# A graph network's edge passes: a third one-hot buffer, gathers one block further ahead, 64 landing counters

## What is computed

```python
x = x + _L0_gnn_ref(h, ..., src, dst)            # sum over edges of H[src] * norm
x = x + _L1_gnn_ref(h, edge_attr_20, edge_weight, src, dst, ...)
x = x + _L2_gnn_ref(h, src, dst, ...)            # 4 rounds: segment_max of message(src)
x = x + _L3_gnn_ref(h, edge_index, ...)          # 2 rounds: segment_sum
...
msg = h[src] * norm[:, None]
out = jax.ops.segment_sum(msg, dst, num_segments=n_nodes)
```

## Time and profile before

| what | value |
|---|---|
| runs | 11399.97, 11347.6, 11393.48 us; median 11393.48 us |
| the profiled execution | 11520.23 us |
| its span, first to last instruction | 11518.5 us |
| mean granted TensorE clock | 0.822 of full |
| busy TensorE / VectorE / GpSimd | 8143.9 / 5554.7 / 6674.3 us |

### The profile page before, as it was taken

How to read it: one execution, slowest core, us unless ns; L and a number is a source line. 1 busy time by engine, 2 the same in 40 slices (tenths; PEclk the granted TensorE clock), 3 DMA queues, 4 the chain that set the end, 5 groups by cost and what they waited for, 6 DMA issues and landing times. The chain is left out here.

```text
span 11518.5 us, 121592 instructions
## 1 busy us (share of the span) xinstructions
PE 8143.9 (71%) x34932; PEld 4146.4 (36%) x35457; DVE 5554.7 (48%) x11902; ACT 820.8 (7%) x2270; POOL 6674.3 (58%) x6440
## 2 busy tenths in 40 slices
PE   4777748888757776677757777477774777667774
PEld 2333237777733332333332333233322333233331
DVE  4455434444445554444545554455544554445554
ACT  2000021111130000100000000100001000010000
POOL 4555568888835555555555555555555555555555
PEclk8888867777778888888878888788887888878887
DMA  4333435555532222222222222222223222322223
GB/s 166 124 129 128 139 88 77 77 77 76 67 106 84 85 85 86 78 80 84 84 81 82 81 85 82 74 85 85 85 84 95 84 85 83 94 79 84 84 83 104
DMA packets 580217, 1042.14 MB, mean 90 GB/s; under 512 B 149064, under 2 KB 419250, under 8 KB 525900
## 3 DMA queue, kind: packets, MB, share of 16 engines
q0 software_dynamic: 298368, 418.22, 17.3%
q1 hardware_dynamic: 278650, 620.49, 15.5%
q10 hardware_dynamic: 2940, 1.00, 0.0%
HBM read 492.11 MB, written 555.62 MB: 91 GB/s over the span
## 5 line engine op out<-in xcount | busy, mean ns | idle before, releaser
L997 POOL DMA_INDIRECT WORK<-table,stage x5124 | 4904.5, 957 | 4178.1 <-DVE WORK L1102 2412.7
L1145 PE MATMUL bank<-TF,XF 128*128 128x512 bf16 x16800 | 5594.1, 414 | 2073.2 <-issue 1029.5
L1080 DVE TENSOR_TENSOR TF<-AF,bank 128x3584 bf16<-128x3584 bf16 x1225 | 2472.3, 2018 | 3645.1 <-remote 2758.8
L1145 PE MATMUL bank<-TF,Z 128*128 128x512 bf16 x8400 | 3467.4, 413 | 181.0 <-issue 176.0
L1145 PEld LDWEIGHTS bank<-TF,XF 128*128 128x128 bf16 x17150 | 1742.5, 104 | 4604.4 <-issue 1902.5
L1312 POOL DMA_INDIRECT acc<-TOT,stage x832 | 1298.0, 1560 | 272.0 <-issue 196.4
L1145 PEld LDWEIGHTS bank<-TF,Z 128*128 128x128 bf16 x8575 | 902.2, 105 | 1410.2 <-issue 577.4
L1102 DVE SCALAR_TENSOR_TENSOR WORK<-WORK,RESET 128x128 f32<-128x128 f32 x2928 | 1028.0, 351 | 352.3 <-DVE WORK L1102 21.3
L1102 DVE SCALAR_TENSOR_TENSOR WORK<-WORK,KEEP 128x128 f32<-128x128 f32 x2196 | 771.2, 351 | 266.0 <-DMA WORK<-table,stage 24.8
L1021 ACT COPY TOT<-bank 128x512 f32<-128x512 f32 x175 | 102.4, 585 | 8486.9 <-PE bank L1145 4343.7
L1517 DVE SCALAR_TENSOR_TENSOR BASE<-bank,WEIGHT,BASE 128x128 f32<-128x128 f32 x832 | 234.1, 344 | 756.4 <-PE bank L1387 721.5
(11 more groups left out here) (249 smaller groups left out, 3089.4 us busy)
## 6 DMA issues: line engine op xcount, KB each, us to landing
run_rows<-WORK SPq DMA_DIRECT2D x357, 1024.0 KB
WORK<-table,stage POOLq DMA_INDIRECT x5124
fill_rows<-BASE SPq DMA_DIRECT2D x52, 1024.0 KB
WORK<-fill_rows SPq DMA_DIRECT2D x104, 512.0 KB
AF<-src_keys SPq DMA_DIRECT2D x175, 128.0 KB
table<-TF SPq DMA_DIRECT2D x56, 384.0 KB
acc<-TOT,stage POOLq DMA_INDIRECT x832
acc<-Z SPq DMA_DIRECT2D x12, 1024.0 KB
```

Source lines behind the costliest of these rows:

```text
L997: pool.indirect_dma_start(RUN[:, b, k, :], None, table, table_row(table, stage[:, b, k:k + 1]))\
L1080: dve.tensor_tensor(OHOT[:, (h * CHUNKS + c) % 2, :, :].rearrange("p k (a e) -> p k a e", e=SPREAD), EKEYS[:, 1 - h, :].rearrange("p (a e) ...
L1145: i = nc.tensor.matmul(bank(2 + h)[:, 0:BATCH], PIECES[n][:, c * PART + k, :], OHOT[:, ((h + 1) * CHUNKS + c) % 2, k, :], start=c + k + n ...
```

## The change

OHOT gets a third buffer, chunk n of a turn of 14 using buffer n % 3. VectorE then waits for the chunk three before (`n - 2`), except for the first two chunks of a turn, where 14 isn't a multiple of 3 and the buffer is that of the chunk two before. GpSimd waits for blocks 0 to c-3 where it waited for blocks 0 to c-2. There are 64 landing counters in place of 32, and each is raised once in a turn.

```diff
--- before.py
+++ after.py
@@ -35,7 +35,7 @@
 E_PAD = P * T
 FULL = E // T
 REST = E - FULL * T
-SLOTS = 32
+SLOTS = 64
 BUFS = 4
 SPAN = BUFS * HALF
 ROUNDS = T // SPAN
@@ -66,8 +66,8 @@
 ONE = 0x3F80
 
 
-assert T % SPAN == 0 and SPAN == 2 * SLOTS
-assert SPAN == 2 * COLS and COLS == SLOTS and PART * CHUNKS == NT and QUAD * CHUNKS <= OWN < COLS
+assert T % SPAN == 0 and SPAN == SLOTS
+assert SPAN == 2 * COLS and PART * CHUNKS == NT and QUAD * CHUNKS <= OWN < COLS
 assert ONE + N_PAD < 0x7F00 and BATCH % SPREAD == 0
 assert sum(SIZES) == NT and max(SIZES) <= GROUP and T % BLOCK == 0 and E < E_PAD
 
@@ -228,7 +228,7 @@
 
         PIECES = [v.bitcast(bf16).rearrange("p (t f) -> p t f", t=NT)
                   for v in (XF[:, 0:NT * F // 2], XF[:, NT * F // 2:NT * F], Z[:, :])]
-        OHOT = TF[:, 0:2 * PART * BATCH // 2].bitcast(bf16).rearrange("p (s k e) -> p s k e", s=2, k=PART)
+        OHOT = TF[:, 0:3 * PART * BATCH // 2].bitcast(bf16).rearrange("p (s k e) -> p s k e", s=3, k=PART)
         KEYS = S[:, 0:NT * SPREAD // 2]
         KEYS_I = S[:, 0:NT * SPREAD // 2].bitcast(i16).rearrange("p (t e) -> p t e", t=NT)
         EKEYS_I = AF[:, 0:BATCH].bitcast(i16).rearrange("p (h e) -> p h e", h=2)
@@ -964,7 +964,7 @@
 
         def turns(k):
 
-            return T // COLS if k < OWN else 1
+            return ROUNDS if k % COLS < OWN else 1 if k < COLS else 0
 
         def passing(maximum, times, pbase, fill=False, back=()):
 
@@ -991,12 +991,12 @@
                             c = it * BUFS + b
                             hold(pool, staged, c + 1)
                             hold(pool, stored[b], it * 16)
-                            hold(pool, reduced, (c - 1) * HALF)
+                            hold(pool, reduced, (c - 2) * HALF)
                         if j % COLS >= OWN and not (first and j < COLS):
                             continue
                         pool.indirect_dma_start(RUN[:, b, k, :], None, table,
                                                 table_row(table, stage[:, b, k:k + 1]))\
-                            .then_inc(landed[j % SLOTS], 16)
+                            .then_inc(landed[j], 16)
                 body(0, first=True)
                 pool.addr_align(256, max_nops=8)
                 with pool.Fori(1, ROUNDS) as it:
@@ -1075,9 +1075,9 @@
                     n = (it * 2 + h) * CHUNKS + c
                     if c == 0:
                         dve.wait_ge(keys_in[1 - h], it * 16 + 16)
-                    wait(dve, oh_used, n - 1)
+                    wait(dve, oh_used, n - 1 if h == 0 and c < 2 else n - 2)
                     shape = [P, PART, BATCH // SPREAD, SPREAD]
-                    dve.tensor_tensor(OHOT[:, (h * CHUNKS + c) % 2, :, :].rearrange("p k (a e) -> p k a e", e=SPREAD),
+                    dve.tensor_tensor(OHOT[:, (h * CHUNKS + c) % 3, :, :].rearrange("p k (a e) -> p k a e", e=SPREAD),
                                       EKEYS[:, 1 - h, :].rearrange("p (a e) -> p a e", e=SPREAD).unsqueeze(1)
                                       .to_broadcast(shape),
                                       keys(c).unsqueeze(2).to_broadcast(shape),
@@ -1094,9 +1094,9 @@
                                 dve.wait_ge(e_turned, it * 2 + h)
                             row = bank(4 + h)[:, (slot - OWN) * P:(slot - OWN + 1) * P]
                         elif slot >= OWN:
-                            dve.wait_ge(landed[slot], base[slot] + 16)
+                            dve.wait_ge(landed[j], base[j] + 16)
                         else:
-                            dve.wait_ge(landed[slot], base[slot] + it * 32 + 16 * (h + 1))
+                            dve.wait_ge(landed[j], base[j] + it * 16 + 16)
                         wait(dve, reduced, t)
                         bp, kp = (b, k - 1) if k else ((b - 1) % BUFS, HALF - 1)
                         dve.scalar_tensor_tensor(RUN[:, b, k, :], RUN[:, bp, kp, :], scale[:, ds(t, 1)],
@@ -1143,7 +1143,7 @@
                         for k in range(PART):
                             for n in range(3):
                                 i = nc.tensor.matmul(bank(2 + h)[:, 0:BATCH], PIECES[n][:, c * PART + k, :],
-                                                     OHOT[:, ((h + 1) * CHUNKS + c) % 2, k, :],
+                                                     OHOT[:, ((1 - h) * CHUNKS + c) % 3, k, :],
                                                      start=c + k + n == 0,
                                                      stop=c == CHUNKS - 1 and k == PART - 1 and n == 2)
                         i.then_inc(oh_used, 1)
```

## The result

The changed kernel takes 12766.40 us (median of 4 runs, 12764.83 to 12774.71) against 11396.72 us of the kernel before (4 runs, 11347.6 to 11461.04): 1.1191 times the time, 95% interval 1.1156 to 1.1226. Forecast were 12890 us and a range from 11450 to 13650. The span of the profiled execution is 12763.1 us, its granted TensorE clock 0.758 of full (before: 0.822).

What follows compares the result with a forecast made beforehand. It took the VectorE-TensorE loop, with TensorE's signals late during gather bursts, as the bound. 7 x (194 + 22) = 1512 us, scaled to 1496, gave 12890 us; range 11450 to 13650.

Steps and rivals of the forecast that it cites:

- The rule of the bursts: During unbroken gathers TensorE's signals come at once for 5 to 8 us, then late; release 39.6 us after the first gather.
- no longer by L1102: Sign of being right: GpSimd's one gap a half ends by ScalarE's staging, not by the wait for reductions.
- Lateness without bursts: Rival: signals come similarly late wherever they fall, so the buffer gains; about 9900 us; chance 0.20 together with unmoved gathers.
- Gathers that don't move: Rival: another wait holds GpSimd's second burst in place, only the buffer works; about 9900 us, counted within the faster 0.20.
- even trade: Rival: burst joined, but chunk 2's signal gets through and slow spells are mild; about 11730 us, chance 0.13.
- The pace: Time of one half, copy to copy: 39.6 + 16.4 + 1.1 = 57.1 us for 49.0, 194 us more a pass.
- TensorE gets chunk 3 done up to then: Step within a half: before the release at 39.6 us TensorE ends chunk 3, leaving chunks 4, 5 and 6.
- lower bound of 52.6: Time of a half in us if TensorE runs all of chunk 4 before the release.
- The start of a pass: 60 gathers without a stop, release at 80.1 us, first copy at 103.0 us for 81.0: 22 us more a pass.
- The end of a pass: Last gathers no longer follow the last copy: gain taken as 0, with 10 us a pass as bound.
- The factor 0.989: Scaling from the profiled execution to plain runs, turning the 1512 us added into 1496 us.
- The counters: Same 28 waits a half on other semaphores, beside comparisons: cost taken as 0.

Runs made afterwards that it cites:

- e6: Changed kernel with each gather from a pass's second turn on replaced by a semaphore increment: 8859.09 us, ratio 0.7723 to the kernel before.
- e12: Changed kernel with each gather from a pass's second turn on replaced by two GpSimd memsets, on chip 8: 8845.71 us, ratio 0.7740 to the kernel before.
- e3: Changed kernel with GpSimd's old wait and two one-hot buffers, leaving only the 64 landing counters: 11438.85 us, ratio 1.0037 to the kernel before.
- e7: Changed kernel where GpSimd begins a half's odd block only after TensorE finished four chunks: 11054.90 us, ratio 0.9646 to the kernel before.
- e1: Changed kernel with GpSimd's old wait put back, leaving the third buffer and the counters: 11845.63 us, ratio 1.0404 to the kernel before.
- e5: Changed kernel fetching 64 bytes a row in place of 512 from a pass's second turn on: 12895.94 us, ratio 1.1244 to the kernel before.

## Why the prediction was right

*The rule of the bursts* held. The comparison of chunk 5 comes 39.4 us after the first gather for 39.6 forecast (39.4 is also the median of the 168 halves with a burst of 28), and 4.4 us behind the end of the gathers for 4.6; e6 and e12 show the cause from the other side. The gap in GpSimd's work is 20.3 us (median) for "some 20". It is ended by staging in 89 of the 175 gaps and still by L1102 in 74. (The list's other 99 waits for L1102 are of 0.3 us, inside a burst.) Whichever it names, the gather starts at the same distance from the copy (5649.74 - 5648.01 = 1.73 and 5705.24 - 5703.44 = 1.80 us), so GpSimd's place is tied to TensorE's seventh chunk as forecast, and the sign "no longer by L1102" was too strict.

*Two rivals fell.* Lateness without bursts (9900 us) is excluded by the pace of 55.4. Gathers that don't move are excluded by the bursts. The *even trade*, chunk 2's signal through and mild slow spells, fell in its first half, since chunk 2's signal was withheld (that is the 22.90 us); of its second half, mild slow spells, a part is true.

*The pace* was over-estimated: 55.4 for 57.1 us. The step that was off is "TensorE gets chunk 3 done up to then". By their starts it runs 79 products between the first gather and the release (the 67, 10 and 4 of the stretches above count two at the edge as well). Chunk 0 had 10 of its 21 behind it at the first gather (it begins at 5647.7), so 74 end chunk 3, and 5 are a quarter of chunk 4. Over the 168 halves it is 2 to 10. What follows the release takes 5703.44 - 5689.18 = 14.3 us for 16.4, and copy to next gather 1.8 for 1.1. Over all 168 halves the means are 38.4 us to the release, 15.3 behind it and 1.8, sum 55.4 (pulled down by some halves in which the signal slips through early). The truth lies between the value taken and the lower bound of 52.6.

*The start of a pass* came out right by two errors that cancel. Third pass, GpSimd's first and last of 60 gathers, VectorE, ScalarE:

```profile
5045.11 0.95 POOL L997 DMA_INDIRECT WORK<-table,stage  x1 [24.69 <-issue]
...
5119.80 0.95 POOL L997 DMA_INDIRECT WORK<-table,stage  x1 [0.30 <-issue]
```

```profile
5129.28 2.02 DVE L1080 TENSOR_TENSOR TF<-AF,bank 128x3584 bf16<-128x3584 bf16 x1 [24.42 <-remote]
```

```profile
5148.56 0.59 ACT L1021 COPY TOT<-bank 128x512 f32<-128x512 f32 x1 [84.76 <-PE bank L1145]
```

The release comes 84.2 us in for 80.1, since it lies 9.5 us behind the start of the last gather where 5.95 was taken; and the rest takes 19.3 us for 22.9. Sum 103.5 (mean of the seven 103.1) for 103.0. *The end of a pass* won 6 us, last copy to last reduction 6.6 for 12.5, inside the bound of 10.

*The sum* on the profiled spans: 7 x 24 x (55.41 - 48.73) = 1122, 7 x 22.1 = 155 for the starts, 7 x 5.9 = 41 off for the ends: 1236 us of the 1244.6 measured. The factor 0.989 was not what the plain runs did: those of the kernel before are 1.1% under its profiled execution, those after are level with theirs (12766.40 and 12764.83), so between plain runs the change costs 1370 us, where the forecast was 1496. Between profiled executions 267 us of the 1512 were too much.

*The counters* were taken as free and cost 0.4% (e3), within the 0.5% that the text called no change.

The prediction set the Trainium skill (SBUF — State Buffer, "Who interferes with whom"), "PE and ACT never wait on anyone", against its reading. That section is on who shares ports to SBUF. Read as saying that TensorE is never slowed by what others do, it doesn't hold on chips 2, 5 and 8, where TensorE's own pace falls to 10 products in 20 us. The late signals are a matter that it doesn't speak of, and no run here shows that a port is behind either. On chip 6 neither is seen: 15.2 us of idle before the comparisons in all.

## What to carry to other kernels

Before two engines are uncoupled so that one may run ahead, look at what the wait between them does for a third: here a wait of GpSimd, for which VectorE hardly ever lacked a row, cut the stream of indirect DMAs, and TensorE's signals passed in the gaps. Buffers and gates are priced together: the third buffer was worth 3 us a half with the cuts held by a gate on the chunk count (e7), and cost 1.6 (50.1 for 48.5 with the counters alone, on the same chip) where it let the cuts vanish (e1). And run a close comparison on more than one chip: the same program differed here by a fifth between chips, and the change costs 12% on one kind and probably nothing on the other.

## What the runs showed of the hardware

- On chips 2, 5 and 8 (and in the traces of before and after, whose chip isn't recorded) TensorE's semaphore signals reach VectorE late while GpSimd issues indirect DMAs without a gap, up to 27.1 us at the longest wait, and TensorE itself falls from one product in 0.22 us (67 in 14.9) to one in 2.0 (10 in 20.2). On chip 6 neither happens, in a burst of 732. What in an indirect DMA does it (its issue, its 128 descriptors or the increments that tell of its landing; not its bytes, by e5), whether the late signals and the slow pace have one cause, and what sets chip 6 apart, is open: the gather's duration, 0.95 us, and the loop of 1.257 us are the same.
- The time of the kernel before on chip 6 is 9074 us, 0.79 to 0.80 of that on the others, with a granted clock of 0.89 for 0.82 to 0.84.
- GpSimd's memset of 128x800 f32 took 766 ns, and the 9408 memsets of e12 disturbed neither TensorE nor its signals.
